# Another order for the edge maps, their roots and the projection quarters in a fused attention and edge-fusion kernel

## The reference, cut to what matters

```python
sobel_h, sobel_v = dwconv(x, K_SX), dwconv(x, K_SY)            # 3x3, per channel
sobel = sqrt(sobel_h ** 2 + sobel_v ** 2 + 1e-08)
lap = abs(dwconv(x, K_LAP))
diag = maximum(abs(dwconv(x, K_D1)), abs(dwconv(x, K_D2)))     # D2 is -D1
grad = sqrt(sobel ** 2 + lap ** 2 + 1e-08)
E = stack([sobel, lap, diag, grad])
y = einsum('kbchw,koc->kbohw', E, w_branch) + b_branch         # four branches, 512 -> 128
feat = gelu(batch_norm(y))
att = sigmoid(gelu(mean(feat) @ w_att1.T + b_att1) @ w_att2.T + b_att2)
z = einsum('bchw,oc->bohw', feat * att, w_fuse) + b_fuse
out = gelu(layer_norm_over_channels(z)) + x
```

## Time and profile before

| | |
|---|---|
| median of 3 runs | 5127.41 us (5125.52 to 5127.98) |
| the profiled execution | 5130.35 us |
| its span, first to last instruction | 5128.5 us |
| TensorE busy | 4844.4 us, 94% of the span |
| DVE busy | 2977.1 us, 58% |
| ScalarE busy | 2237.4 us, 44% |
| GpSimd busy | 1253.4 us, 24% |
| mean granted TensorE clock | 0.977 |

### The profile page before, as it was taken

How to read it: one execution, slowest core, us unless ns; L and a number is a source line. 1 busy time by engine, 2 the same in 40 slices (tenths; PEclk the granted TensorE clock), 3 DMA queues, 4 the chain that set the end, 5 groups by cost and what they waited for, 6 DMA issues and landing times. The chain is left out here.

```text
span 5128.5 us, 68411 instructions
## 1 busy us (share of the span) xinstructions
PE 4844.4 (94%) x23784; PEld 3445.3 (67%) x23784; DVE 2977.1 (58%) x4115; ACT 2237.4 (44%) x4183; POOL 1253.4 (24%) x1030
## 2 busy tenths in 40 slices
PE   8999999999999999999999997999999989998968
PEld 7887888888888888888888883344444434443423
DVE  4554554554554554544554541885688578848865
ACT  3443443443443343443443430554555455545545
POOL 2442442432432332342342330000300020011003
PEclk9999999999999999999999998999999999999969
DMA  6666666666666666656656645443434344434313
GB/s 186 201 217 204 201 221 204 206 215 204 205 207 211 208 198 212 209 195 216 208 192 222 209 156 188 134 148 113 142 132 153 108 141 132 151 116 142 110 33 116
DMA packets 390816, 893.21 MB, mean 174 GB/s; under 512 B 33488, under 2 KB 66512, under 8 KB 388240
## 3 DMA queue, kind: packets, MB, share of 16 engines
q1 hardware_dynamic: 390544, 889.18, 52.5%
HBM read 588.74 MB, written 300.32 MB: 173 GB/s over the span
## 5 line engine op out<-in xcount | busy, mean ns | idle before, releaser
L775 POOL TENSOR_TENSOR toeplitz<-taps 128x512 f32<-128x512 f32 x768 | 912.2, 1215 | 905.9 <-PE bank L458 905.9
L458 PE MATMUL bank<-toeplitz,columns 128*128 128x128 f32 x8192 | 956.4, 276 | 0.0
L1083 PE MATMUL bank<-att,w_proj 128*128 128x512 f32 x2048 | 906.3, 597 | 47.7 <-DMA att<-att_dram 36.9
L458 PEld LDWEIGHTS bank<-toeplitz,columns 128*128 128x128 f32 x8192 | 938.8, 192 | 0.0
L1083 PEld LDWEIGHTS bank<-att,w_proj 128*128 128x128 f32 x2048 | 393.3, 192 | 542.4 <-issue 503.7
L367 PE MATMUL bank<-x_hi,w_hi 128*128 128x512 f32 x1536 | 613.8, 400 | 22.9 <-DVE x_lo L628 22.9
L1427 POOL TENSOR_TENSOR centred<-centred,x_out 128x512 f32<-128x512 f32 x128 | 164.6, 1320 | 1909.8 <-ACT centred L1235 1909.8
L369 PE MATMUL bank<-x_lo,w_hi 128*128 128x512 f32 x1536 | 602.0, 392 | 0.0
L1096 PE MATMUL bank<-edge,w_branch 128*128 128x512 f32 x1024 | 503.3, 640 | 102.5 <-ACT edge L1186 102.5
L368 PE MATMUL bank<-x_hi,w_lo 128*128 128x512 f32 x1536 | 600.0, 391 | 0.0
L628 DVE TENSOR_TENSOR x_lo<-x_sb,x_hi 128x1536 fp32r<-128x1536 f32 x128 | 250.7, 1959 | 413.8 <-ACT x_hi L502 413.8
(11 more groups left out here) (122 smaller groups left out, 7102.0 us busy)
## 6 DMA issues: line engine op xcount, KB each, us to landing
x_sb<-in_x_tiled SPq DMA_DIRECT2D x128, 1024.0 KB, 6.4
tiles_dram<-tiles SPq DMA_DIRECT2D x128, 867.0 KB, 7.3
loaded<-tiles_dram SPq DMA_DIRECT2D x256, 433.5 KB, 4.0
inverse<-inverse_dram SPq DMA_DIRECT2D x256, 256.0 KB, 5.1
att_dram<-out_sb SPq DMA_DIRECT2D x256, 256.0 KB, 4.2
att<-att_dram SPq DMA_DIRECT2D x64, 1024.0 KB, 6.2
xb<-x_dram SPq DMA_DIRECT2D x128, 330.0 KB, 3.1
x_out<-in_x_pad SPq DMA_DIRECT2D x32, 1056.0 KB, 5.2
```

What stands on the lines that cost most here:

```text
L458: last = nc.tensor.matmul(bank[:, v * M:(v + 1) * M], columns[:, h % 2, t - T_K, v + b, a * HT:(a + TO) * HT], w[:, t, d, :], start=(d == ...
L775: last = nc.gpsimd.tensor_tensor(toeplitz[:, h % 2, t, :].rearrange("p (d o r) -> p d o r", o=HD, r=PL), tap, point, ALU.mult)
L1083: last = nc.tensor.matmul(P_BANKS[m][:, :], w_proj[:, i * HALF + k, m * P:(m + 1) * P], att[:, i, k, :], start=(i == 0 and k == 0), stop=( ...
```

## The change

There are four edits, all of order. TensorE: in a step that is not fresh, the branch of quarter k stands behind projection quarter k + 1, not behind quarter k, as it did already in the fresh step. So P0 B0 P1 B1 P2 B2 P3 B3 becomes P0 P1 B0 P2 B1 P3 B2 B3, and the leaving step, P0 B0 P1 B1 P2 B2 B3 P3, becomes P0 P1 B0 P2 B1 B2 B3 P3. ScalarE: the roots of the quarter before come first, then the gradients, then the diagonal, then the Laplacian. DVE: the two sums of the quarter before stand behind dx and behind smooth, and the diagonal, with its wait for `branched`, behind sobel_h. ScalarE and DVE: the roots and sums of a chunk's last quarter move from the end of its step into quarter 0 of the next step, or into `drain` behind the last chunk of an image.

```diff
@@ TensorE, step
-                        if mj is not None and k - fresh in range(KT):
+                        if mj is not None and k >= 1:
...
-                            branch(*mj, k - fresh)
+                            branch(*mj, k - 1)
@@ ScalarE, step and drain
                     for k in range(KT):
-                        diagonal(KT * u + k + 1, k % 2)
-                        if k >= 1:
+                        if k >= 1 or prev_m is not None:
                             roots(KT * u + k, (k - 1) % 2)
                         gradients(KT * u + k + 1, k % 2)
+                        diagonal(KT * u + k + 1, k % 2)
                         laplacian(u, k, k % 2)
                         if k == 0 and prev_m is not None:
                             features(*prev_m)
-                    roots(KT * u + KT, (KT - 1) % 2)
...
                     else:
+                        roots(KT * chunk(b, NCH), (KT - 1) % 2)
                         features(b, NCH - 1)
@@ DVE, stencils
-                def stencils(b, j, k):
+                def stencils(b, j, k, follows):
...
                     nc.vector.tensor_tensor(dx, x[:, :, 2:W2], x[:, :, 0:W], ALU.subtract).then_inc(done["dx"], 1)
+                    if follows:
+                        sums(n - 1, 1 - s, 0)
...
                                                    op0=ALU.mult, op1=ALU.add).then_inc(done["smooth"], 1)
+                    if follows:
+                        sums(n - 1, 1 - s, 1)
                     dve.wait_ge(done["dx"], n)
-                    dve.wait_ge(branched, START + n - 2)
-                    nc.vector.tensor_tensor(maps_of[:, 2, :, :], dx[:, 2:XR, :], dx[:, 0:CR, :], ALU.subtract).then_inc(done["diag"], 1)
                     nc.vector.tensor_tensor(sobel_h[:, s, :, :], dx[:, 2:XR, :], dx[:, 0:CR, :], ALU.add).then_inc(done["rows"], 1)
-                    if k >= 1:
-                        sums(n - 1, 1 - s, 0)
...
-                    if k >= 1:
-                        sums(n - 1, 1 - s, 1)
...
                                                    in1=sobel_h[:, s, :, :], op0=ALU.mult, op1=ALU.add).then_inc(done["sobel_h"], 1)
+                    dve.wait_ge(branched, START + n - 2)
+                    nc.vector.tensor_tensor(maps_of[:, 2, :, :], dx[:, 2:XR, :], dx[:, 0:CR, :], ALU.subtract).then_inc(done["diag"], 1)
@@ DVE, step and drain
-                            stencils(*mj, k)
+                            stencils(*mj, k, k >= 1 or prev_m is not None)
...
-                    if mj is not None:
+
+                def drain(p, b):
+                    if b is not None:
                         for part in range(2):
-                            sums(KT * chunk(*mj) + KT, (KT - 1) % 2, part)
-
-                def drain(p, b):
+                            sums(KT * chunk(b, NCH), (KT - 1) % 2, part)
```

## The result

The changed kernel takes 5074.95 us (median of 4 runs, 5073.12 to 5077.47), the kernel before 5126.47 on the same chip: a ratio of 0.9904, 95% interval 0.9887 to 0.9921. The profiled execution took 5073.12 us with a span of 5070.7; TensorE is now busy for 95% of it, at a mean granted clock of 0.982.

The account below looks back on a forecast made before the run. TensorE, 94% busy, was held to lose time only to idle and low clock, waiting for `edges` in 29 places. -14.3 - 23.2 - 7.7 + 18.4 - 26.7 = -53.5 gave 5073.9 us; bounds 5065 to 5080.

Parts of the forecast that it names:

- Loop steps: Loop steps: two projection quarters cover the chain to B0, so its waits go, 14.3 us and 23.2 in first loop steps.
- B3's chain in ordinary steps: From the end of B1 to B3: 8.65 us of hand-overs against 10.30 of cover, 1.65 left, so no wait.
- Rival B: B3's chain exceeds its cover in ordinary steps by about 1 us: +29 us, 5103; chance 0.08.
- the Trainium skill's drain: Loop heads: about 1.38 us added to each table load would make B3 0.3 late in 8 heads, 3 us more.
- The fresh step: Fresh steps: DVE skips diagonal, rows and sobel_v before B0, 6.24 becoming 4.31; 1.93 x 4 = 7.7 us gained.
- The open clause: Fresh steps, images 1 and 2: if shorter idle keeps the clock up, each wins 2.84, loses about 1 at B3; up to 11.4.
- The leaving step: Three images' last step with projection: only B2 covers B3's chain, so idle 3.2 and a slow group; +18.4 us, or +9.9.
- The tail: Last three steps, branches only: DVE's 7.87 per quarter sets the pace; 118.85 us becomes 92.1, gain 26.7.
- A: The clock stays up wherever it was taken as fallen: 69 us gained in all, 5058; chance 0.12.
- C: DVE starts the next chunk before this one's last sums, so late `xb` rows hold back B3: +87, 5161; chance 0.05.
- D: The waits at B0 only move to B1 or B2, time within 0.2% (10 us): 5127; chance 0.03.

Follow-up runs that it names:

- the long probe: The changed kernel with one extra DVE reciprocal of 512 elements, 3.35 us, ahead of side of quarter 0 in loop and cross-image steps: 5118.59 us.
- the Gelus ahead: The changed kernel with ScalarE's Gelus of the chunk before put ahead of quarter 0's Laplacian in the three steps without a projection: 5072.86 us.
- unchained: The changed kernel with the sums and roots of a chunk's last quarter put back at the end of its own step: 5068.86 us.

## Why the prediction held, point by point

**Loop steps: right.** The waits at B0 are gone, 14.3 and 23.3 us. ScalarE's timeline after, the head of the loop step at 3330.43 and the chain behind B1, and the start of the tail:

```profile
3335.60 1.28 ACT L1183 ACT_TABLE_LOAD   x1
3336.90 0.72 ACT L1183 ACTIVATE edge<-sobel_v,edge_eps 128x512 f32<-128x512 f32 x1
...
3364.27 0.72 ACT L1183 ACTIVATE edge<-sobel_v,edge_eps 128x512 f32<-128x512 f32 x1 [2.24 <-DVE sobel_v L1305]
...
3365.61 0.72 ACT L1186 ACTIVATE edge<-lap_sq,edge_eps 128x512 f32<-128x512 f32 x1 [0.61 <-DVE lap_sq L1309]
...
4825.97 0.63 ACT L1177 ACTIVATE lap_sq<-edge 128x512 f32<-128x512 f32 x1 [1.43 <-DVE edge L1342]
...
4827.12 1.28 ACT L1192 ACT_TABLE_LOAD   x1
4828.42 0.78 ACT L1192 ACTIVATE feat<-bank,bn_shift,bn_scale 128x512 f32<-128x512 f32 x1
```

**B3's chain in ordinary steps: right.** B1 ends at 3357.90, the second root at 3366.33: 8.43 where the steps gave 8.6 without TensorE's start. B3 stands at 3368.20 as the second half of the x16, 1.9 later; the long probe puts the slack at 1.9 too. Rival B is dead by these. DVE's timeline after, the diagonal in that step, and in the tail the sides of quarters 1 and 2 and the two diagonals that wait:

```profile
3358.10 0.69 DVE L1337 TENSOR_TENSOR edge<-work 128x512 f32<-128x512 f32 x1 [2.34 <-PE bank L1096]
...
4858.66 0.82 DVE L1318 TENSOR_TENSOR work<-xb 128x640 f32<-128x640 f32 x1
...
4866.53 0.82 DVE L1318 TENSOR_TENSOR work<-xb 128x640 f32<-128x640 f32 x1
...
4872.97 0.69 DVE L1337 TENSOR_TENSOR edge<-work 128x512 f32<-128x512 f32 x1 [1.04 <-PE bank L1096]
...
4906.38 0.69 DVE L1337 TENSOR_TENSOR edge<-work 128x512 f32<-128x512 f32 x1 [1.74 <-PE bank L1096]
```

**The table load: the traces decide against the drain.** The load at 3335.60 takes 1.28 us and the next root starts at 3336.90. No load is repeated at a loop head: the tables for roots and Gelus are loaded 32 times each in the edge part's steps, before and after. So the 3 us by the Trainium skill's drain ("ScalarE: Activation LUTs", "What ACT_TABLE_LOAD costs") aren't there. The load for the Gelus did stand behind a wait for TensorE in the loop steps of before; after, it is done before that wait.

**The fresh step: the mechanism right, the size at its upper end.** From DVE's quarter 1 to B0 each is 1.94 shorter (6.24 to 4.30), where 1.93 was worked out. The open clause came true: B0 now follows idles of 1.78 and 1.85 in images 1 and 2 and runs at full clock, 3.70 where 6.30 and 5.40 stood, and B3 waits 0.64. With image 3's group 1.1 shorter and image 0's 0.3 longer that is 3.3 us, on top of 7.7. The other 1.7 is mostly the projection at the start of image 0, which the change doesn't touch: its first twelve quarters take 84.15 for 85.52, and the mean clock up to the two quarters ahead of B0 is 0.98 where it was 0.96.

**The leaving step: the mechanism right, its size 3.8 too high.** Idle is 3.05 for 3.2; the group lost 1.80 and not 2.84. The windows show why: the stretch of idle still has a granted clock of 1.00, and the group behind it 0.68 on average, so a part of it ran at the upper of the two levels.

**The tail: the step that failed.** The first chunk was right: B3 at +28.7, its end at +32.2, both as forecast. The step at fault is "In a further step, counted from the B3 before ... B3 at 12.4 + 2.65 + 7.87 + 4.31 = 27.2", with a fast B3 ending at 30.8. From B3 to B3 that makes 30.8, but DVE alone has four quarters of 7.87 to do in between, 31.5. I had counted the chain by its waits only and never held it against DVE's own pace, though the paragraph's first sentences say that DVE sets it. The wrong term is the diagonal: I had it at 10.9, held to 12.4 by B0. But DVE begins quarter 1 only as B3 ends (4858.66), so it can't be at quarter 2's diagonal before 13.1, and started it at 14.3 (4872.97). With the forecast's other terms, 14.3 + 2.65 + 7.87 + 4.31 = 29.2, which is where B3 stands. Measured from start to start: 4855.09 to 4887.80 is 32.7, that is 31.5, 1.04 for the wait of that diagonal, and 0.2. B3 then ran slowly as well (5.40), so the chunk ended at +34.4, not 30.8. The last one took 30.3 for 29.1, with a diagonal that waits 1.74 (4906.38). B0 came 7.9, 8.5 and 6.8 after the B3 before, not 6.0: ScalarE's Gelus stand behind quarter 0's Laplacian, for which it waits 1.43 (4825.97), and only then comes the table load (4827.12). In the tail of before the load ran during the wait for B3 (4858.85, B3 ending at 4862.38). This is the reason for the 1.04: with the Gelus ahead no diagonal waits. It isn't the reason for the pace: that kernel gains only 0.9, as DVE then waits for the Laplacian's square instead.

**Rivals.** A (the clock stays up wherever I took it as fallen) came partly true: in images 1 and 2 of the fresh step, not in the leaving step or the tail, whose mean clock is 0.79. The Trainium skill, "TensorE: Matmul & The Clock Gate", Part 1, has the clock follow how busy the engine has been. The traces agree: in the tail TensorE's busy share is 0.58 and its clock 0.79, in the loop window 1.00 and 1.00. Slow and full groups alternate nearly as taken: in the second chunk B2 ran at full speed and B3 slowly, the other way round. C (late rows) is dead: DVE's only wait for rows is the 6.3 of before. The rows are issued at 3336.45, 6.0 into the step where I had expected 10.5. SP's write of x2 did move, from 2.2 ahead of the step (3336.40 before) to 1.1 into it (3331.50), but the rows' issue didn't move with it: before, it stood 8.7 behind the write, now 5.0. SP's queue after:

```profile
3336.45 3.21 SPq L980 DMA_DIRECT2D xb<-x_dram  x2
```

D is dead by the loop window. What the prediction didn't ask is which of the two halves does the work: nearly all of it is the order of the maps. Within it, the diagonal's place is worth 15 us and chaining none; the places of the two sums and ScalarE's order weren't tried by themselves, so what each gives of the tail's 21.9 stays open.

## What to carry to other kernels

Where a change holds two remedies for one wait, cost each alone as well: here they overlap, and one of them gives back in a single step (the leaving one) what it gains elsewhere. When a chain of hand-overs is summed between two equal points of a cycle, hold the sum against each engine's own work in that cycle; the longer one counts. Here DVE's wait for a free buffer was better placed behind the work that others wait for (15 us). After such a move the place of each group in the step must be read again wherever cover is thin.

## What the runs showed of the hardware

- The same idle of 2.88 us was followed by a group of 5.40 (three times in the changed kernel, once unchained) and by one of 3.70 (twice unchained). Idles of 1.78 to 1.85 were followed by full speed. The length of the idle doesn't decide alone: in the changed kernel's tail 3.57 was followed by 3.70, and 4.17 by 5.40.
- The fall comes inside the group behind an idle stretch, not in it: 1.00 over 3526.10 to 3529.10, then 0.68 to 3534.40. A group of eight costs 1.80 more then, against 2.70 and 2.84 where the clock over the group was 0.58 and 0.57 (the groups of 6.30 and 6.44 in the kernel before).
- The same attention code ends anywhere between 3102 and 3115 us, and single executions of the kernel before lie between 5112 and 5133. Two executions of the changed kernel have edge parts of 1960.2 and 1961.5, so a change there is read more closely from the trace, counted from the start of the changed part.
